# A graph network on one core: fourteen groups gathered by TensorE, single-width picks, a two-tensor one-hot

## The reference, cut to what matters

```
# layer 0: a maximum over the edges of each destination
msgs = z[dst] @ Wd + z[src] @ Ws + edge_weight[:, None] * ww + bm
agg  = segment_max(msgs, dst)              # 0 where a node has no edge
x    = layernorm(z + relu(z @ W1a + agg @ W1b + b1) @ W2 + b2)
# layer 1: the mean over the edges of each destination, twice
mean = segment_sum(x[src], dst) / max(degree, 1)
h    = relu(mean @ W1l.T + b1l + x @ W1r.T)
out  = layernorm(x + mean_of(h) @ W2l.T + b2l + h @ W2r.T)
```

## Time and profile before

| | |
|---|---|
| median of three runs | 1105.2 us (1101.52 to 1110.27) |
| the profiled execution | 1106.44 us, span 1104.6 us |
| mean granted TensorE clock | 0.973 |
| PE busy, of the span | 1024.0 us, 93% |
| DVE, ACT, POOL busy | 850.7, 669.8, 737.7 us |

### The profile page before, as it was taken

The page is one execution under the profiler, slowest core; times in us unless marked ns, Lnnn a source line. Parts: engine busy times, 40 slices in busy tenths (PEclk is TensorE's granted clock), DMA queues, the critical chain, the costliest instruction groups (busy, mean ns, idle before and its releaser), DMA issues.

```text
span 1104.6 us, 25686 instructions
## 1 busy us (share of the span) xinstructions
PE 1024.0 (93%) x7179; PEld 757.5 (69%) x7179; DVE 850.7 (77%) x2994; ACT 669.8 (61%) x1739; POOL 737.7 (67%) x782
## 2 busy tenths in 40 slices
PE   4768999999999999999999999998898998899997
PEld 4456777777777677776767777666566676657786
DVE  6577988788878887886888788987887877645465
ACT  3234789888977787877877888533333333313664
POOL 7667777777777777777776777777777777200332
PEclk9798899999999999999999999999999999999999
DMA  8553344344443443444343433443453454445221
GB/s 204 156 138 94 92 105 106 91 103 115 97 103 106 102 112 96 99 98 129 96 120 85 102 94 98 126 124 88 101 148 93 112 145 103 144 126 161 83 58 42
DMA packets 127867, 121.29 MB, mean 110 GB/s; under 512 B 24094, under 2 KB 112469, under 8 KB 127717
## 3 DMA queue, kind: packets, MB, share of 16 engines
q1 hardware_dynamic: 101288, 70.53, 24.3%
q0 software_dynamic: 23328, 47.82, 17.8%
q10 hardware_dynamic: 3101, 1.21, 0.4%
HBM read 105.60 MB, written 13.88 MB: 108 GB/s over the span
## 4 chain that ended last, share of the span: by engine, by line
PE 55%; POOL 13%; issue 11%; ACT 7%; DVE 5%; SPq 3%; DMA 3%; ACTq 2%; DVEq 0%
POOL area L1084 13%; PE bank L1817 10%; PE bank L1719 9%; PE bank L1942 7%; PE bank L1708 6%; PE bank L1786 5%; PE bank L1659 5%; PE bank L1698 4%; PE bank L1647 3%; ACT area L938 2%; PE bank L1907 2%; ACT hot_r L946 2%; ACT area L891 1%; ACTq L878 1%; PE bank L1893 1%
## 5 line engine op out<-in xcount | busy, mean ns | idle before, releaser
L1084 POOL DMA_INDIRECT area<-zs_d,area x709 | 685.4, 967 | 227.8 <-issue 215.0
L885 ACT CAST adj_w<-bank 128x325 f32 x391 | 176.7, 452 | 320.0 <-PE bank L1719 251.7
L1270 DVE TENSOR_TENSOR_SCAN area<-area,bank 128x512 f32<-128x512 bf16 x196 | 249.6, 1274 | 148.7 <-PE bank L1659 122.7
L1254 DVE TENSOR_SCALAR area<-area 128x325 bf16<-128x325 f16 x782 | 250.5, 320 | 0.0
L1719 PE MATMUL bank<-area 128*128 128x104 f32 x1564 | 226.1, 288 | 0.3
L1253 DVE TENSOR_SCALAR area<-area 128x128 bf16<-128x128 f16 x782 | 210.6, 269 | 8.5 <-PE bank L1719 8.4
L1719 PEld LDWEIGHTS bank<-area 128*128 128x128 f32 x1564 | 196.8, 198 | 10.7 <-issue 2.2
L1817 PE MATMUL bank<-hot_r,zs_r 128*128 128x512 f32 x600 | 176.8, 421 | 3.0 <-ACT hot_r L946 2.2
L1708 PE MATMUL bank<-area 128*128 128x325 bf16 x782 | 151.6, 307 | 9.8 <-DVE area L1255 5.5
L938 ACT ACTIVATE area<-adj_w,node_c 128x512 bf16<-128x512 f32 x225 | 156.5, 744 | 0.0
L1659 PE MATMUL bank<-ident,area 128*128 128x128 f32 x714 | 119.2, 290 | 17.0 <-DMA area<-zs_d,area 16.8
(11 more groups left out here) (175 smaller groups left out, 1081.1 us busy)
## 6 DMA issues: line engine op xcount, KB each, us to landing
area<-mask_d SPq DMA_DIRECT2D x195, 128.0 KB
area<-zs_d,area POOLq DMA_INDIRECT x709
area<-zs_d SPq DMA_DIRECT2D x640, 0.5 KB
area<-parts_d SPq DMA_DIRECT2D x20, 384.0 KB, 7.5
area<-wp_d SPq DMA_DIRECT2D x195, 9.0 KB
adj_w<-in_src_dram SPq DMA_DIRECT2D x12, 256.0 KB
zr_d<-area SPq DMA_DIRECT2D x24, 128.0 KB
area<-zr_d SPq DMA_DIRECT2D x6, 512.0 KB, 4.8
```

Of the source, the lines that this page charges most:

```text
L885: nc.scalar.copy(adj[:, :, bass.ds(at, W)], A_BANK[s % 2][:, 0:COLS].rearrange("p (h w) -> p h w", w=W))
L1084: pool.indirect_dma_start(gring[:, g % GR * 4 + s % 2 * 2 + u, :], None, x if g < RAW else zs_d[0:N, :], bass.IndirectOffsetOnAxis(ap=firs ...
L1254: nc.vector.tensor_scalar(hot_d[:, r, u, :], i_key[:, 0:COLS], key_n[:, u, s:s + 1], None, ALU.is_equal)
L1270: nc.vector.tensor_tensor_scan(S[:, g % 2, 0:n], mask[:, g % MR, 0:n], (G_BANK if g in PICKED else T_BANK[g % 2])[:, 0:n], S[:, (g + 1) % ...
```

## The change

It does three things.

- `PICKS` was a list of twelve pairs, nine slots apart up to group 55 and eleven after that, with 143 as the last. It becomes fourteen pairs, nine slots apart throughout, from 28 to 145.
- The picks of segment ends stream their 13 columns once, not eight times.
- DVE's source one-hot compares two tensors: the node number is broadcast along the row as a second tensor, where before it was a scalar operand.

```
-WIDE = 8
-PICKS = ((28, 19), (37, 28), (46, 37), (55, 46), (66, 55), (77, 66), (88, 77), (99, 88), (110, 99), (121, 110), (132, 121), (143, 132))
+PICKS = tuple((a + 9, a) for a in range(19, 145, 9))
...
-                    nc.vector.tensor_scalar(hot_r[u % HOTS], keys[i % 2], node_c[:, h:h + 1], None, ALU.is_equal).then_inc(hot_vec, 1)
+                    nc.vector.tensor_tensor(hot_r[u % HOTS], keys[i % 2], node_c[:, h:h + 1].unsqueeze(2).broadcast_to([P, 4, P]), ALU.is_equal).then_inc(hot_vec, 1)
...
-                            last = nc.tensor.matmul(o[:, 384:384 + WIDE * W].rearrange("p (n w) -> p n w", w=W), St[:, b * P:(b + 1) * P],
-                                                    sel[:, g % 2, u, s % 2, :].unsqueeze(1).broadcast_to([P, WIDE, W]),
+                            last = nc.tensor.matmul(o[:, 384:384 + W], St[:, b * P:(b + 1) * P],
+                                                    sel[:, g % 2, u, s % 2, :],
                                                     start=u == 0, stop=u == 1)
```

## The result

| | before | after |
|---|---|---|
| median of six runs each | 1105.96 us | 1137.53 us (1133.09 to 1147.6) |
| profiled execution, span | 1106.44, 1104.6 us | 1141.83, 1140.0 us |
| mean granted clock of that execution | 0.973 | 0.943 |

The ratio is 1.0297, with an interval of 1.0264 to 1.0331: 31.6 us slower. The forecast was 1121 us, and its range ended at 1135. The direction was right and the size was not. Of all runs in this document one, of e13 (1150.91 us), lay over 1.5% above the fastest of its kernel; the ratios leave it out and the medians hold it.

A forecast was written before the change was run, and what follows sets the result against it. It took PE as the bound while rows are picked and gathers after, nearly balanced. The picks added 14.2 us to 1106.4, with narrowing, compares, ACT and SP at nothing: 1120.6, forecast 1121 us, range 1096 to 1135.

The forecast's parts named there:

- What bounds the kernel: Whole kernel: PE has no time left while rows are picked, gathers limit after 698 us; the two are balanced within microseconds.
- The added picks: Between 126 us and group 145: 100 more matmuls give PE 22.3 us more work, of which 14.2 us reach the end.
- The narrow picks: Segment picks, eight passes a group: the float32 weight load sets their 0.12 us each, so 13 columns save zero.
- its rival: Groups 19 to 144: narrow picks free PE and gathers set the pace, 1096 us or some microseconds less; chance 0.2.
- The clock rival: Picking stretch: narrow picks stream less, PE's clock falls in half of 24 stretches, 21 us on top, 1142 us; chance 0.08.
- The signs that were set: If right: loads 0.11 us apart, POOL's waits 20 us or more, group 142's scan near 713 us, last gather near 961.
- The sign for the clock rival: Picking stretch: a granted clock below 0.95 there would mean that the clock had fallen.
- The argument against that rival: Picking stretch: the added row picks stream 512 columns each, set against the clock falling there.
- The compares, at nothing: DVE's one-hots: two-tensor compares of 0.692 us add 23.9 us to DVE, costed at nothing in the total time.
- the cover: Picking stretch: 67 DVE scans waited 69.7 us for PE, about 1 us each against 0.21 us more per one-hot.
- ACT and SP, at nothing: ACT's 38 more one-hots, 52.6 us at most, and SP's two more rows of source numbers cost nothing.
- The sum: Whole kernel: 19.5 us more PE work before group 142, less POOL's 5.3 us lag, adds 14.2 us: 1120.6 us.

The follow-up runs named there:

- e13: The change plus 20 bfloat16 products of 512 columns ahead of PE's wait for the weights of group 10: 1136.03 us, ratio 1.0246.
- e1: The kernel before with only the fourteen picks; eight-fold columns and the scalar compare stay: 1118.17 us, ratio 1.0117.
- e4: The change with eight-fold columns put back in the segment picks: 1121.04 us, ratio 1.0147.
- e14: The kernel before plus 20 bfloat16 products of 512 columns ahead of PE's wait for the weights of group 10: 1105.46 us, ratio 1.0012.
- e3: The kernel before with only the two-tensor compare: 1108.18 us, ratio 1.0031.
- e2: The kernel before with only the narrow segment picks; twelve picks and the scalar compare stay: 1116.02 us, ratio 1.0100.
- e5: The change with segment picks of groups 0 to 16 eight-fold again, later ones narrow: 1128.26 us, ratio 1.0219.
- e9: The change with segment picks narrow in groups 0 to 16 and eight-fold in all later ones: 1125.41 us, ratio 1.017.
- e5 to e9: The change with, in turn: early picks wide, early products added, 52-column picks, scalar compare, later picks wide: 1128.26, 1140.29, 1124.11, 1136.54, 1125.41 us.

## Why the prediction was wrong, point by point

- **What bounds the kernel: right.** The kernel before stands at the balance of PE and POOL: one picked group less costs 4.3 us, two more cost 13.8.
- **The added picks, 14.2 us: right.** e1 measured 13.8, with group 142 at 712.3 us and the last gather at 961.3.
- **The narrow picks, "I take zero": this step failed.** The half that I argued was right: passes of 104, 52 and 13 columns are bound by the weight load, eight in 0.97 us. But I asked only what the passes cost, and put the loss "by way of the clock" aside at 0.08. With the wide streams the granted clock was 0.84 and 1.00 in the two long stages (e4), without them 0.62 and 0.97: beside fourteen groups, narrowing cost 14.9 us with the load spacing unchanged. Of the traces that differ in this alone, 9.2 us came before group 19, a stretch that the terms on narrowing and its rival left out, although the clock of 0.80 from 100 to 125 us stood in the earlier trace rows. The clock rival too was worked out for the picking stretch only, as 21 us there; 13.0 were seen. From 80 to 126 us the kernel before has slack on PE, because POOL issues its gathers there without waiting for it (e14); in the change, with narrow picks, POOL waits for PE's transposes six times between 40 and 130 us, where it waited once (before, then after):

```profile
POOL area L1084 <- PE bank L1659: 3.0, 1, 3.0
```

```profile
POOL area L1083 <- PE bank L1658: 6.7, 6, 3.7
```

- **The signs that were set.** Loads 0.11 us apart and a longer wait of POOL came. Group 142 and the last gather came some 20 us later than the sum, at 733.4 and 982.3 us. The sign for the clock rival, a clock below 0.95 in the picking stretch, did not come, although the loss goes with the clock: it was 0.97 there, and 0.62 from 40 to 126 us, where no sign had been set.
- **The argument against that rival**, that the row picks stream 512 columns each, was no reason: before group 19 there are no row picks at all, and behind it the clock fell beside them (0.80 from 550 us).
- **The compares, at nothing: mis-sized by 3 to 4 us.** The operation takes 0.681 us, near the 0.692 that I took, so what failed is the cover: DVE's 69.7 us of waits did not hide all of it. Where it is lost was not found: in the traces group 145's scan comes no later in e4 (725.3 us) than in e1 (726.5). The mean clock does not show it either, with 0.977 in e3 and 0.981 in e4.
- **ACT and SP, at nothing: right** as far as shown; PE waits 8.3 us for one-hots where it waited 8.5.
- **The sum.** Along e1, e4 and the change it is 13.8 for the picks, 2.9 for the compares and 14.9 for the narrowing, where I had 14.2, 0 and 0. The parts do not simply add, since narrowing costs less beside twelve groups. A reason that fits, argued and not isolated: in e2 34 of the 120 us at 1.2 GHz between 40 and 960 us fall after 700 us, where gathers set the pace; in the change it is 17 of the same 120.

The clock as the cause rests on four things: the loads' spacing did not change; the same thirty groups take no longer narrow than wide where the clock is 1.00 in both, and twenty take 5.7 us longer where it falls; in e5 and e9 the runs with the lower clock are the slower ones, but for one pair that is nearly even; and in e13 the clock came back for 17 us during and behind streams that widen no pass. No run kept the clock up for the whole of a narrow kernel, so the full 14.9 us were not bought back without width. The Trainium skill, "TensorE: Matmul & The Clock Gate", section "HAM oscillation — how this bites in real kernels", warns of long idle gaps on PE. The change's fall at 81.5 us fits it, in the midst of 5.2 us in which PE stood idle. The falls between 170 and 720 us follow idle times of 0.8 us at most, and the 25 us of gapless PE that stayed at 1.2 GHz are not in that section. Why the clock falls there with narrow streams and not with wide ones stays open.

## What to carry to other kernels

Streams that hide under weight loads look free to remove, and are not if the clock falls without them, as it did here: where a cut leaves the spacing of instructions as it is, compare the granted clock of each stage before counting it as zero. Read the clock beside the busy share, since a PE at half speed shows as fuller, not emptier. Cost a part in every stage that runs it, also in those where the rest of the change does nothing.

## What the runs showed of the hardware

- Weight loads follow the clock: eight float32 loads take 0.97 us at 2.4 GHz and 1.83 us at 1.2 GHz.
- A PE that is busy without a gap may stay at 1.2 GHz: for all of the 25 us from 100 us in the change (granted clock 0.50), and for nearly all of the 20 us from 126 us in e13 (0.51). Earlier in e13 the clock came back at 87.4 us, within a run of 512-column bfloat16 products that began at 82.7 us.
- Float32 passes with 13 columns cost nothing over 104 columns at full clock: thirty groups took 143.7 and 144.6 us at 1.00.
- Beside fourteen groups the time of one program varies more when its passes are narrow: 5.7 us or more from lowest to highest in each of e5 to e9, and 2.0 us in e1 and in e4.
